# Gated delta rule on one core: inversion blocks on four tiles, recurrence by batch, taps and scaling at other places

## The chip, the core and the metric

One Trainium2 chip, one of its cores. The time is device microseconds (us) of one launch of the kernel. Engines: TensorE (PE; its weight loads are PEld), VectorE (DVE), ScalarE (ACT), GpSimd (POOL) and the queue of SyncE (SP), each with a program of its own, written out by hand, and tied to the others by semaphores.

## The reference

```python
xn = _layernorm(x)                          # x: 4 x 512 x 256
qkv, z, b, a = projections of xn            # 16 key heads, 32 value heads of 128
qkv = silu(causal depthwise conv of 4 taps)
beta = sigmoid(b); g = -exp(A_log) * softplus(a + dt_bias)
# per value head, chunks of 64 positions, g summed within the chunk:
decay = where(tril, exp(g_i - g_j), 0)
M = where(stril, (k_beta @ k.T) * decay, 0)
T = solve_triangular(eye + M, eye)          # inverse of a 64 x 64 matrix
v_c, k_cumdecay = T @ v_beta, T @ (k_beta * exp(g))
# scan over the 8 chunks:
v_new = v_i - kcd_i @ state
out_i = (q_i * exp(g_i)) @ state + attn @ v_new
state = state * exp(g_last) + (k_i * exp(g_last - g_i)).T @ v_new
h = norm_w * rmsnorm(out) * silu(z);  s = h @ W_out.T
y = x + s * silu(ffn of lookup weights)(xn)
```

## The kernel before

The head computes the layer norm, the gates and the first round's inputs; then come 32 rounds, and the feed-forward part as a tail. A round is one key head and two of the four batches (`BB` = 2), so two value heads per batch (`RATIO` = 2), which lie in the two halves of the 128 partitions: a chunk's 64 x 64 matrix of value head 0 in partitions 0 to 63, of value head 1 in 64 to 127. All matmuls are float32; the profile records each as two loads and two matmuls, so 32 matmuls are 64 records. Each engine runs `body(R)`, unrolled six times in a loop of five passes, plus two last rounds; in the last one (`nxt` is False) nothing is prepared for a following round.

The stages of a round on TensorE:

- `invert`: five levels (`LEVELS` - 1). In each, block p1 (`products`: U times W, W is X transposed), then a side matmul, then block p2 (P1 times X), then another (`beside`). The side work of levels 1 to 4 is the projections of the next round, eight in all (`PROJ_AT`: 0 and 1 in level 1, 2 and 3 in level 2, and so on), that of level 5 the gate projections z.
- ScalarE copies p1's result to P1. VectorE copies p2's result into X where a mask says so (`copy_predicated`, in place), and `turn` transposes X into W by 32 x 32 blocks for the next level.
- The projections are raw inputs of the convolution. A kind is two projections, for two batches: kinds 0 to 3 are projections (0, 1), (2, 3), (4, 5), (6, 7). ScalarE's `tap0` writes the first tap to `cacc`, VectorE's `taps` adds three more, reading the projection's bank each time, and then releases both banks; ScalarE's `silu` follows.
- `keys_through`: key products (L475), and the last z.
- `recur`: eight chunks. Kg times state (L510) is added to the old part (L484), VectorE scales it to Vn (L923), Kd times Vn (L537) goes to the state banks, GpSimd's decayed state Sd is added (L931) to give the next St; new part (L490) and qg times state (L518) give the output o. Every two chunks a quarter of the output is ready: ScalarE squares it, GpSimd's `norm` makes its factor, VectorE's `scale_o` multiplies (L943), TensorE's `turn_back` transposes it (L557), VectorE's `gated` multiplies with z (L954).
- `begin` of the following round: kkq products (L422), transposes of k (L430) and v (L435); then `outputs` (L567).

PSUM has eight banks, with a full and a read semaphore each. `bank_uses` lists who uses which bank in a round, in order: a writer waits (`wait_open`) until the use before its own is read. Banks 0, 1, 6, 7 take the projections in turn: projections 0 and 4 share bank 0, 2 and 6 share bank 6. z 0 comes after projection 4 in bank 0. An engine issues in the order of its program, so what stands behind a waiting instruction waits too.

```python
TURN_AT = {3: 0, 5: 1, 7: 2}
PROJ_AT = {lv: (2 * lv - 2, 2 * lv - 1) for lv in range(1, 5)}
```

## Time and profile before

| | |
|---|---|
| median of 3 runs | 3193.22 us |
| lowest, highest | 3192.94, 3195.3 us |
| the profiled execution: its time | 3193.03 us |
| the profiled execution: its span | 3191.2 us |
| TensorE's granted clock, mean over the span | 0.988 |
| one round (first block to first block of the next) | 91.18 us |

Busy times count an engine's own instructions; TensorE's are pipelined and their ends modelled, so starts are what to subtract. In brackets behind a row of a timeline stands how long the engine was idle before it and what released it; DVEq is VectorE's sequencer, which sends a semaphore on. The rounds repeat: the one from 1499.44 to 1590.62 us stands for 31, the last is shown by its own rows.

### The profile page before, as it was taken

The numbers are of one execution on the slowest core, as the hardware profiler recorded it, in microseconds if no ns is written. First come the engines' busy times: TensorE is split into PE (matmuls) and PEld (weight loads), VectorE is DVE, ScalarE is ACT, GpSimd is POOL, SyncE is SP. The second block draws the span as 40 slices with busy tenths as digits, with TensorE's granted clock in tenths as the row PEclk, the third lists the DMA queues.
The fourth block names the chain that finished last, engine by engine and source line by source line (L and its number), as shares of the span: only waits on it lengthen the run. The fifth ranks groups of instructions, "written<-read, shape, count | busy, mean of one in ns | idle before, by whom it ended". The sixth has DMA issues, their size and how long they took to land.

```text
span 3191.2 us, 101541 instructions
## 1 busy us (share of the span) xinstructions
PE 2911.1 (91%) x41680; PEld 2122.0 (66%) x41680; DVE 1643.1 (51%) x2807; ACT 1305.7 (41%) x3046; POOL 1782.0 (56%) x1829
## 2 busy tenths in 40 slices
PE   2899999999999999999999999999999999999889
PEld 1566766766667666667766667677666667766744
DVE  4555555555555555655555555555545655555412
ACT  2443444444444444444444444444444444444311
POOL 1565555656655565665555566655555665555500
PEclk7899999999999999999999999999999999999999
DMA  2111110110111001011110101111011111110020
GB/s 83 27 30 29 30 22 19 27 35 24 30 29 27 20 22 34 24 30 29 30 29 9 35 24 30 30 29 31 13 29 27 29 29 29 30 25 9 3 61 20
DMA packets 71088, 89.52 MB, mean 28 GB/s; under 512 B 16720, under 2 KB 39376, under 8 KB 70608
## 3 DMA queue, kind: packets, MB, share of 16 engines
q1 hardware_dynamic: 70608, 82.74, 10.1%
q8 instruction: 347, 5.69, 0.8%
q14 instruction: 133, 1.09, 0.1%
HBM read 77.64 MB, written 5.08 MB: 26 GB/s over the span
## 4 chain that ended last, share of the span: by engine, by line
issue 35%; POOL 32%; PE 19%; DVE 7%; ACT 2%; POOLq 1%; DVEq 0%; DMA 0%; SPq 0%
POOL hT L1071 10%; POOL hT L1077 5%; PE ps L422 4%; POOL Kd L1094 4%; PE ps_state L537 3%; DVE St L931 3%; PE ps L510 3%; POOL Dm L1012 2%; POOL Sd L1035 2%; POOL Dm L1009 2%; PE ps L557 2%; POOL Kg L1094 2%; PE ps L611 2%; POOL A L1101 1%; PE ps_two L601 1%
## 5 line engine op out<-in xcount | busy, mean ns | idle before, releaser
L1035 POOL TENSOR_TENSOR Sd<-St,el 128x512 f32<-128x512 f32 x192 | 201.3, 1048 | 897.2 <-DVE St L928 843.4
L411 PEld LDWEIGHTS ps<-XW,U 64*64 64x64 f32 x10240 | 317.9, 135 | 125.8 <-issue 123.8
L411 PEld LDWEIGHTS ps<-XW,P 64*64 64x64 f32 x10240 | 311.8, 135 | 119.8 <-issue 119.8
L1071 POOL TENSOR_SCALAR hT<-idx_s,lutb 128x134 f32<-128x134 int32 x480 | 355.4, 744 | 27.5
L411 PE MATMUL ps<-XW,U 64*64 64x64 f32 x10240 | 342.9, 220 | 17.2 <-issue 12.7
L411 PE MATMUL ps<-XW,P 64*64 64x64 f32 x10240 | 333.6, 220 | 0.0
L834 DVE SCALAR_TENSOR_TENSOR cacc<-ps_two,cw,cacc 128x1022 f32<-128x1022 f32 (+2 forms) x192 | 245.7, 1280 | 97.1 <-ACT cacc L638 92.5
L923 DVE TENSOR_TENSOR Vn<-ps,bR 128x256 f32<-128x256 f32 x256 | 108.6, 424 | 350.3 <-PE ps L484 296.7
L834 DVE SCALAR_TENSOR_TENSOR cacc<-ps_state,cw,cacc 128x1022 f32<-128x1022 f32 (+2 forms) x192 | 245.7, 1280 | 78.5 <-ACT cacc L638 73.9
L382 PE MATMUL ps_two<-xnT,w_qkv 128*128 128x512 f32 x512 | 261.8, 636 | 20.4 <-DVEq L838 18.5
L711 ACT ACTIVATE P<-ps 128x512 f32<-128x512 f32 x320 | 184.2, 595 | 229.9 <-PE ps L411 229.3
L382 PE MATMUL ps_state<-xnT,w_qkv 128*128 128x512 f32 x512 | 253.3, 618 | 1.3 <-DVEq L838 1.3
L910 DVE COPY_PREDICATED XW<-cst,ps 128x256 f32<-128x256 int32 x320 | 158.4, 495 | 183.8 <-issue 167.8
L894 DVE STREAM_TRANSPOSE XW<-XW 128x512 f32<-128x512 f32 x320 | 227.7, 711 | 40.5 <-DVE XW L910 9.7
L402 PE MATMUL ps_two<-xnT,w_z 128*128 128x512 f32 x512 | 245.4, 612 | 0.0
L931 DVE TENSOR_TENSOR St<-Sd,ps_state 128x512 f32<-128x512 f32 x192 | 131.9, 687 | 200.1 <-PE ps_state L537 163.9
L567 PE MATMUL ps_two<-w_o,hT 128*128 128x256 f32 x1024 | 226.3, 379 | 0.0
L567 PEld LDWEIGHTS ps_two<-w_o,hT 128*128 128x128 f32 x1024 | 192.1, 190 | 24.8
L510 PE MATMUL ps<-St,Kg 128*64 128x128 f32 x1792 | 146.7, 284 | 58.8 <-DVE St L931 58.6
L537 PE MATMUL ps_state<-Vn,Kd 64*128 64x128 f32 x1792 | 160.3, 295 | 35.4 <-DVE Vn L923 29.9
L422 PE MATMUL ps<-kq 128*128 128x128 f32 x1024 | 132.2, 283 | 62.5 <-DVEq L947 46.6
L738 ACT ACTIVATE P<-ps 128x128 f32<-128x128 f32 x256 | 67.2, 277 | 295.2 <-PE ps L490 295.2
(140 smaller groups left out, 5552.7 us busy)
## 6 DMA issues: line engine op xcount, KB each, us to landing
qg<-g_scratch SPq DMA_DIRECT2D x64, 512.0 KB, 7.4
g_st<-g_scratch SPq DMA_DIRECT2D x64, 256.0 KB, 5.7
w_qkv<-in_wqkvz SPq DMA_DIRECT2D x16, 512.0 KB, 3.8
w_z<-in_wqkvz SPq DMA_DIRECT2D x16, 256.0 KB, 3.1
w_o<-in_wout SPq DMA_DIRECT2D x16, 256.0 KB, 3.3
idx_s<-in_idx SPq DMA_DIRECT2D x32, 67.0 KB, 1.8
fw_scratch<-looked_up SPq DMA_DIRECT2D x32, 67.0 KB, 1.9
Kg<-in_x SPq DMA_DIRECT2D x2, 1024.0 KB, 7.6
```

The costliest lines, as they stand in the source:

```text
L382: m = pe.matmul(bank[:, :], w_qkv[:, k, kind * P:(kind + 1) * P], xnT[:, k, cols(par, b)], start=(k == 0), stop=(k == KD - 1))
L402: m = pe.matmul(bank[:, :], w_z[:, k, a * P:(a + 1) * P], xnT[:, k, cols(R.par, b)], start=(k == 0), stop=(k == KD - 1))
L411: m = pe.matmul(bank[r, c * C:(c + 1) * C], left[r, b, c, :], right[r, b, c, :], start=True, stop=True)
L422: m = pe.matmul(bank[:, u * P:(u + 1) * P], kq[:, i // 2, c, 0:P], kq[:, i // 2, c, C:3 * C], start=True, stop=True)
L510: m = pe.matmul(bank[r, b * P:(b + 1) * P], Kg[:, b, c, r], St[:, cur, b, a, :], start=False, stop=True, skip_group_check=True)
L537: m = pe.matmul(ps[6 + a][:, b * P:(b + 1) * P], Kd[r, b, c, :], Vn[r, cur, b, :], start=True, stop=True)
L567: m = pe.matmul(bank[:, b * D:(b + 1) * D], hT[:, t, b, 1 - a, :], w_o[:, a, :], start=(a == 0), stop=(a == RATIO - 1))
L834: dve.scalar_tensor_tensor(dst, both[n][:, :, 0:S - t], cw[:, kind, 3 - t:4 - t], dst, ALU.mult, ALU.add).then_inc(s["taps"], 1)
L894: dve.transpose(W[:, b].rearrange("p c i -> p (c i)"), X[:, b].rearrange("p c i -> p (c i)")).then_inc(xs, 1)
L931: dve.tensor_tensor(St[:, 1 - cur, :, :, :], Sd[:, :, :, :], part, ALU.add).then_inc(done, 1)
L1035: pool.tensor_tensor(Sd[:, :, :, :], St[:, c % 2, :, :, :], el[:, R.par, :, :, c].unsqueeze(3).broadcast_to([P, BB, RATIO, P]), ALU.mult). ...
L1071: m = pool.tensor_scalar(slots[k], idx_s[:, :], float(k), lutb[:, k:k + 1], ALU.is_equal, ALU.mult)
```

## The change

- `products` issues both batches in one block, on four tiles of 64 x 64. In p1 batch 1 goes to the off-diagonal tiles, so its result lies in swapped halves; p2 takes it from there, and needs X of batch 1 in swapped halves too: the new tile Xs, which ScalarE's `swap` copies (two copies of 64 partitions) after each level's update of X.
- P1's copy, the predicated copy and the transpose cover both batches in one instruction.
- VectorE's `taps` of a kind run one level later (levels 2 to 5, not 1 to 4), ScalarE's `silu` too, the last behind gate 3. The projections stay in their levels and banks.
- In the recurrence each batch has its own bank and its own signals: Vn is two instructions (`tensor_scalar`), the state add two (semaphore `st_c`), and TensorE waits for each batch by itself.
- `scale_o` goes between Vn and the state add of chunks 3, 5, 7, `gated` into the same gap of chunks 4 and 6 and, for the third quarter, into `begin`; `turn_back` stands at the end of chunks 3, 5 and 7. In `begin` scale_o of the last quarter follows all four kkq.
- The mask table `masks` is twice as wide (loaded once, in the head). Banks: kkq in 4 to 7, kt and vt spread over 2 to 7, p1 in 2 and 3, p2 in 4 and 5, outputs o in 2 and 3, their transposes in 1.
- GpSimd: `with_beta` in chunks 1 and 3, `first_level` in 5 and 6, `lengths` (the pow that makes rinv) behind the loop.

VectorE, levels 1 and 2 of a round, before (cacc is written by the taps, with kind 0 in ps_two and kind 1 in ps_state):

```order
L910 COPY_PREDICATED XW<-cst,ps 128x128x2
L911 REGISTER_ALU
L894 STREAM_TRANSPOSE XW<-XW 128x512
L828 ISA
L834 SCALAR_TENSOR_TENSOR cacc<-ps_two,cw,cacc 128x2x511
L832 ISA
L834 SCALAR_TENSOR_TENSOR cacc<-ps_two,cw,cacc 128x2x510
L832 REGISTER_ALU
L834 SCALAR_TENSOR_TENSOR cacc<-ps_two,cw,cacc 128x2x509
L836 REGISTER_ALU
L214 REGISTER_ALU
L909 MEMSET carry 128x1
```

and with the change:

```order
L931 COPY_PREDICATED XW<-cst,ps_p 128x256x2
L933 ISA
L920 STREAM_TRANSPOSE XW<-XW 128x1024
L219 REGISTER_ALU x2
L930 MEMSET carry 128x1
L931 COPY_PREDICATED XW<-cst,ps_p 128x128x4
L933 REGISTER_ALU
L920 STREAM_TRANSPOSE XW<-XW 128x1024
L850 ISA
L856 SCALAR_TENSOR_TENSOR cacc<-ps_two,cw,cacc 128x2x511
```

The taps of kind 0 stood behind level 1's transposes and stand now behind level 2's.

TensorE in chunk 3, before (L557 is turn_back):

```order
L220 REGISTER_ALU
L510 MATMUL ps<-St,Kg 64x128 x4
L518 MATMUL ps<-St,qg 64x128 x4
L557 MATMUL ps<-cst,on 128x2x64 x4
L537 MATMUL ps_state<-Vn,Kd 128x128 x4
L490 MATMUL ps<-Vn,A 64x128
```

and with the change, end of chunk 3 and start of chunk 4 (L501 is the new part, L496 the old, L571 turn_back, L523 Kg times state, L531 qg times state; each L213, L220 or L520 is a wait's number being worked out):

```order
L501 MATMUL ps_p<-Vn,A 64x128
L496 MATMUL ps_p<-V,XW 64x128
L213 REGISTER_ALU
L571 MATMUL ps_two<-cst,on 128x2x64 x4
L520 REGISTER_ALU
L523 MATMUL ps_p<-St,Kg 64x128 x2
L520 REGISTER_ALU
L523 MATMUL ps_p<-St,Kg 64x128 x2
```

The Kg products are two by two, each pair with its wait, and turn_back moved from ahead of the Kd products (L537) to the chunk's end, ahead of the next Kg products.

```diff
-TURN_AT = {3: 0, 5: 1, 7: 2}
+SCALE_AT = {3: 0, 5: 1, 7: 2}
+GATE_AT = {4: 0, 6: 1}
 PROJ_AT = {lv: (2 * lv - 2, 2 * lv - 1) for lv in range(1, 5)}
...
+    begin = (spread([("kkq", i) for i in range(4)], (4, 5, 6, 7)) + spread([("kt", i) for i in range(4)], (2, 4, 5, 6))
+             + spread([("vt", i) for i in range(4)], (3, 7, 2, 4)))
+    levels = []
     for lv in range(1, LEVELS):
-        wide += [("p1", (lv, b)) for b in range(BB)] + [("p2", (lv, b)) for b in range(BB)]
+        levels += spread([("p1", (lv, b)) for b in range(BB)], (2, 3)) + spread([("p2", (lv, b)) for b in range(BB)], (4, 5))
+    small = spread([("z", i) for i in range(4)] + (N2 if nxt else []), (0, 1))
     keys = spread([("kcd", i) for i in range(4)], (4, 5, 6, 7))
-    outs = [("o", 0), ("o", 1), ("ot", 0), ("o", 2), ("ot", 1), ("o", 3), ("ot", 2)]
-    steps = spread([("vn", c) for c in range(NC)] + [("ot3", 0)], (5,)) + spread([("sp", c) for c in range(NC - 1)], (6,))
-    return ahead + spread(small, (0, 1)) + spread(wide, (2, 3, 4)) + keys + spread(outs, (2, 3, 4)) + steps
+    steps = spread([("vn", n) for n in range(NC * BB)], (4, 5)) + spread([("sp", c) for c in range(NC - 1)], (6,))
+    outs = spread([("o", i) for i in range(4)], (2, 3)) + spread([("ot", i) for i in range(4)], (1,))
+    return begin + ahead + levels + small + keys + steps + outs + spread([("out", i) for i in range(4)], (0, 1))
...
-            def products(bank, b, left, right):
...
                 for c in range(NC):
                     for a in range(RATIO):
-                        r = slice(a * C, (a + 1) * C)
-                        m = pe.matmul(bank[r, c * C:(c + 1) * C], left[r, b, c, :], right[r, b, c, :],
-                                      start=True, stop=True)
-                return m
+                        same, other = slice(a * C, (a + 1) * C), slice((1 - a) * C, (2 - a) * C)
+                        cols = slice(c * C, (c + 1) * C)
+                        if first:
+                            left = pe.matmul(banks[0][0][same, cols], U[same, 0, c, :], W[same, 0, c, :], start=True, stop=True)
+                            right = pe.matmul(banks[1][0][other, cols], U[same, 1, c, :], W[same, 1, c, :],
+                                              start=True, stop=True)
+                        else:
+                            left = pe.matmul(banks[0][0][same, cols], P1[same, 0, c, :], X[same, 0, c, :],
+                                             start=True, stop=True)
+                            right = pe.matmul(banks[1][0][same, cols], P1[other, 1, c, :], Xs[other, c, :],
+                                              start=True, stop=True)
+                left.then_inc(banks[0][1], 1)
+                right.then_inc(banks[1][1], 1)
...
-                if last is not None:
-                    turn_back(last, 3)
...
                     m.then_inc(filled, 1)
+                if last is not None:
+                    turn_back(last, 3)
...
                 for lv in range(1, LEVELS):
-                    for b in range(BB):
-                        pe.wait_ge(s["xs"], R.at(3 * (b + 1) if lv == 1 else 6 + (lv - 2) * 4 + 2 * (b + 1), 0, 24))
-                        bank, filled = wait_open(pe, R, "p1", (lv, b))
-                        products(bank, b, U, W).then_inc(filled, 1)
+                    pe.wait_ge(s["xs"], R.at(2 * lv, 0, 11))
+                    products([wait_open(pe, R, "p1", (lv, b)) for b in range(BB)], True)
                     beside(R, lv, 0)
                     for b in range(BB):
                         wait_read(pe, R, "p1", (lv, b))
-                        bank, filled = wait_open(pe, R, "p2", (lv, b))
-                        products(bank, b, P1, X).then_inc(filled, 1)
+                    pe.wait_ge(s["x_c"], R.at(2 * lv, 0, 10))
+                    products([wait_open(pe, R, "p2", (lv, b)) for b in range(BB)], False)
                     beside(R, lv, 1)
...
+                olds = []
                 for b in range(BB):
...
                         m = old_part(R, 0, a, b, bank)
+                    m.then_inc(filled, 1)
+                    olds.append((bank, filled))
                 for c in range(NC):
                     cur = c % 2
-                    if c:
-                        wait_read(pe, R, "sp", c - 1)
                     for b in range(BB if c else 0):
+                        pe.wait_ge(s["st_c"], R.at(2 * (c - 1) + b + 1, 0, 2 * (NC - 1)))
                         for a in range(RATIO):
                             r = slice(a * C, (a + 1) * C)
-                            m = pe.matmul(bank[r, b * P:(b + 1) * P], Kg[:, b, c, r], St[:, cur, b, a, :], start=False,
+                            m = pe.matmul(olds[b][0][r, 0:P], Kg[:, b, c, r], St[:, cur, b, a, :], start=False,
                                           stop=True, skip_group_check=True)
-                    m.then_inc(filled, 1)
+                        m.then_inc(olds[b][1], 1)
...
-                    if c in TURN_AT:
-                        turn_back(R, TURN_AT[c])
...
-                    wait_read(pe, R, "vn", c)
                     if c < NC - 1:
-                        bank, filled = wait_open(pe, R, "vn", c + 1)
                         _, s_filled = wait_open(pe, R, "sp", c)
                         for b in range(BB):
+                            wait_read(pe, R, "vn", c * BB + b)
...
+                                old_part(R, c + 1, a, b, olds[b][0])
...
+                    if c in SCALE_AT:
+                        turn_back(R, SCALE_AT[c])
...
+                swap(R, 0)
...
-                    for b in range(BB):
-                        bank, done = wait_full(act, R, "p1", (lv, b))
-                        src = bank[:, :].rearrange("p (c t) -> p c t", t=C)
-                        act.activation(P1[:, b], src, ACT.Copy).then_inc(done, 1)
-                    if lv < 5:
+                    done = [wait_full(act, R, "p1", (lv, b))[1] for b in range(BB)]
+                    act.activation(P1[:, :, :, :].rearrange("p b c t -> p b (c t)"), ps_p1[:, :, :], ACT.Copy
+                                   ).then_inc(done[0], 1)
+                    wait_read(act, R, "p1", (lv, 0))
+                    act.sem_inc(done[1], 1)
+                    if R.nxt and lv > 2:
+                        silu(R, lv - 3)
+                    if lv < LEVELS - 1:
+                        swap(R, lv)
                         if R.nxt:
-                            if lv > 1:
-                                silu(R, lv - 2)
                             tap0(R, lv - 1)
                     else:
-                        if R.nxt:
-                            silu(R, 3)
                         gate(R, 0)
                         gate(R, 1)
...
+                act.wait_ge(s["xs"], R.at(1 + 2 * lv, 0, 11))
+                for a in range(RATIO):
+                    act.activation(Xs[(1 - a) * C:(2 - a) * C], X[a * C:(a + 1) * C, 1], ACT.Copy).then_inc(s["x_c"], 1)
...
+                    silu(R, 3)
...
                 for i in range(4):
                     if i == 2 and last is not None:
-                        scale_o(last, 3)
+                        gated(last, 2)
...
+                if last is not None:
+                    scale_o(last, 3)
                 for b in range(BB):
-                    if b and last is not None:
-                        gated(last, 3)
                     dve.wait_ge(s["u_c"], R.at(2 * b + 2, 0, 4))
-                    dve.tensor_tensor(X[:, b], X[:, b], over_chunks(eye), ALU.add).then_inc(xs, 2)
-                    dve.wait_ge(xs, R.at(3 * b + 2, 0, 24))
-                    turn(b)
+                over_all = eye.unsqueeze(1).broadcast_to([P, BB * NC, C])
+                x_all = X[:, :].rearrange("p b c i -> p (b c) i")
+                dve.tensor_tensor(x_all, x_all, over_all, ALU.add).then_inc(xs, 1)
+                if last is not None:
+                    gated(last, 3)
+                dve.wait_ge(xs, R.at(1, 0, 11))
+                turn()
...
                 for lv in range(1, LEVELS):
+                    done = [wait_full(dve, R, "p2", (lv, b))[1] for b in range(BB)]
...
+                    dve.memset(carry[:, 1:2], 0.0)
+                    dve.copy_predicated(odd(flat(X)), masks[lv - 1].rearrange("p (q n) -> p q n", n=n).bitcast(I32),
+                                        odd(flat(ps_p2))).then_inc(xs, 1)
+                    dve.wait_ge(xs, R.at(1 + 2 * lv, 0, 11))
                     for b in range(BB):
...
-                        dve.memset(carry[:, 1:2], 0.0)
-                        dve.copy_predicated(dst, mask.bitcast(I32), src).then_inc(xs, 1)
-                        dve.wait_ge(xs, R.at(22 + b + 1 if lv == LEVELS - 1 else 6 + (lv - 1) * 4 + 2 * b + 1, 0, 24))
-                        dve.sem_inc(done, 1)
-                        if lv < LEVELS - 1:
-                            turn(b)
-                    if R.nxt and lv < 5:
-                        taps(R, lv - 1)
+                        dve.sem_inc(done[b], 1)
+                    if lv < LEVELS - 1:
+                        turn()
+                    if R.nxt and lv > 1:
+                        taps(R, lv - 2)
...
-                    bank, done = wait_full(dve, R, "vn", c)
-                    src = bank[:, 0:BB * P].rearrange("p (b e) -> p b e", e=P)
-                    dve.tensor_tensor(Vn[:, cur], src, per_chunk(bR[:, R.par, :, c], P), ALU.mult).then_inc(done, 1)
+                    for b in range(BB):
+                        bank, done = wait_full(dve, R, "vn", c * BB + b)
+                        dve.tensor_scalar(Vn[:, cur, b], bank[:, 0:P], bR[:, R.par, b, c:c + 1], None,
+                                          ALU.mult).then_inc(done, 1)
+                    if c in SCALE_AT:
+                        scale_o(R, SCALE_AT[c])
+                    if c in GATE_AT:
+                        gated(R, GATE_AT[c])
                     if c < NC - 1:
                         _, done = wait_full(dve, R, "sp", c)
-                        part = ps_state[:, :, 0:BB * P].rearrange("p a (b e) -> p b a e", e=P)
-                        if c == 0:
-                            dve.tensor_copy(St[:, 1, :, :, :], part).then_inc(done, 1)
-                        else:
+                        if c:
                             dve.wait_ge(s["sd_c"], R.at(c, 0, NC - 2))
-                            dve.tensor_tensor(St[:, 1 - cur, :, :, :], Sd[:, :, :, :], part, ALU.add).then_inc(done, 1)
+                        for b in range(BB):
+                            part, dst = ps_state[:, :, b * P:(b + 1) * P], St[:, 1 - cur, b, :, :]
+                            if c == 0:
+                                dve.tensor_copy(dst, part).then_inc(s["st_c"], 1)
+                            else:
+                                dve.tensor_tensor(dst, Sd[:, b, :, :], part, ALU.add).then_inc(s["st_c"], 1)
+                        dve.wait_ge(s["st_c"], R.at(2 * c + 2, 0, 2 * (NC - 1)))
+                        dve.sem_inc(done, 1)
                     if c == 0 and R.nxt:
                         lengths(R)
-                    if c in (2, 4, 6):
-                        scale_o(R, c // 2 - 1)
-                    if c in TURN_AT:
-                        gated(R, TURN_AT[c])
...
+                    gated(R, 2)
...
                     decayed_state(R, c)
-                    if c == 1 and R.nxt:
-                        lengths(R)
                     if c % 2 == 0:
                         norm(R, c // 2 - 1)
-                    if R.nxt and c <= BB:
-                        with_beta(R, c - 1)
-                    elif R.nxt and c <= 2 * BB:
-                        first_level(R, c - 1 - BB)
+                    if R.nxt and c in (1, 3):
+                        with_beta(R, c // 2)
+                    elif R.nxt and c > 4:
+                        first_level(R, c - 5)
+                if R.nxt:
+                    lengths(R)
                 norm(R, 3)
```

## Rows read from the trace of the kernel before

**Rows 1.** The page: its first line, and busy time by engine.
```profile
span 3191.2 us, 101541 instructions
...
PE 2911.1 (91%) x41680; PEld 2122.0 (66%) x41680; DVE 1643.1 (51%) x2807; ACT 1305.7 (41%) x3046; POOL 1782.0 (56%) x1829
```

**Rows 2.** Timeline of TensorE, one round: start us, us, engine line op tiles, xcount [idle before].
```profile
1499.44 2.08 PE L411 MATMUL ps<-XW,U 64*64 64x64 f32 x64
1501.45 1.98 PE L382 MATMUL ps_two<-xnT,w_qkv 128*128 128x512 f32 x4
1503.36 2.08 PE L411 MATMUL ps<-XW,P 64*64 64x64 f32 x64
...
1536.99 3.70 PE L402 MATMUL ps_two<-xnT,w_z 128*128 128x512 f32 x8
1540.62 2.00 PE L475 MATMUL ps<-XW,Kg 64*128 64x64 f32 x32
...
1551.95 0.64 PE L510 MATMUL ps<-St,Kg 128*64 128x128 f32 x8
...
1573.28 2.05 PE L422 MATMUL ps<-kq 128*128 128x128 f32 x16 [0.32 <-DVEq L957]
1576.83 2.05 PE L422 MATMUL ps<-kq 128*128 128x128 f32 x16 [1.50 <-DVEq L947]
...
1583.12 0.66 PE L435 MATMUL ps<-cst,vs 128*128 128x128 f32 x4 [0.36 <-ACT V L702]
```

**Rows 3.** Timeline of VectorE, levels 1 and 2 of that round.
```profile
1504.57 0.73 DVE L910 COPY_PREDICATED XW<-cst,ps 128x256 f32<-128x256 int32 x1 [4.34 <-issue]
...
1508.59 3.91 DVE L834 SCALAR_TENSOR_TENSOR cacc<-ps_two,cw,cacc 128x1022 f32<-128x1022 f32 x3 [0.91 <-ACT cacc L638]
1512.85 0.43 DVE L910 COPY_PREDICATED XW<-cst,ps 128x256 f32<-128x256 int32 x1 [0.35 <-DVE cacc L834]
...
1513.43 0.71 DVE L894 STREAM_TRANSPOSE XW<-XW 128x512 f32<-128x512 f32 x1
```

**Rows 4.** Timeline of TensorE, the recurrence: two records on other tiles, and the next group.
```profile
1549.63 0.27 PE L490 MATMUL ps<-Vn,A 64*64 64x128 f32 x1
...
1549.65 0.27 PE L484 MATMUL ps<-V,XW 64*64 64x128 f32 x1
1549.74 0.27 PE L490 MATMUL ps<-Vn,A 64*64 64x128 f32 x1
```

**Rows 5.** Timeline of all engines, levels 1 and 2 of the last round.
```profile
2973.38 0.71 DVE L894 STREAM_TRANSPOSE XW<-XW 128x512 f32<-128x512 f32 x1
...
2974.24 1.15 PE L411 MATMUL ps<-XW,U 64*64 64x64 f32 x32 [0.84 <-DVE XW L894]
...
2975.42 0.60 ACT L711 ACTIVATE P<-ps 128x512 f32<-128x512 f32 x1 [3.32 <-PE ps L411]
```

**Rows 6.** Timeline of TensorE, chunk 4 and the start of chunk 5.
```profile
1561.75 0.66 PE L510 MATMUL ps<-St,Kg 128*64 128x128 f32 x8 [0.27 <-DVE St L931]
...
1563.03 0.71 PE L537 MATMUL ps_state<-Vn,Kd 64*128 64x128 f32 x8 [0.19 <-DVE Vn L923]
...
1564.62 0.66 PE L510 MATMUL ps<-St,Kg 128*64 128x128 f32 x8 [0.27 <-DVE St L931]
```

**Rows 7.** Timeline of VectorE, chunk 4.
```profile
1562.51 0.42 DVE L923 TENSOR_TENSOR Vn<-ps,bR 128x256 f32<-128x256 f32 x1
1563.88 0.69 DVE L931 TENSOR_TENSOR St<-Sd,ps_state 128x512 f32<-128x512 f32 x1 [0.94 <-PE ps_state L537]
```

**Rows 8.** Timeline of GpSimd, the pow that makes rinv.
```profile
1552.43 2.92 POOL L1051 TENSOR_TENSOR rinv<-kn,cst 128x16 f32<-128x16 f32 x1 [1.02 <-DVE kn L852]
```

**Rows 9.** Timeline of TensorE, in the head.
```profile
24.73 1.97 PE L350 MATMUL ps_two<-cst,V 128*128 128x128 f32 x8 [3.41 <-DVE xnT L780]
```

**Rows 10.** Stretches of the head: length, busy time by engine, TensorE's granted clock (PEclk), DMA.
```profile
24.00:28.00 4.00, 3.27 (x15) 2.81 (x16) 2.87 (x6) 0.00 (x0) 0.00 (x0) 1.00 0.00 0
...
40.00:44.00 4.00, 0.00 (x0) 0.00 (x0) 3.82 (x3) 1.40 (x2) 0.00 (x0) 0.50 0.00 0
```

**Rows 11.** The page: the costliest groups, the product blocks on TensorE.
```profile
L411 PE MATMUL ps<-XW,U 64*64 64x64 f32 x10240 | 342.9, 220 | 17.2 <-issue 12.7
L411 PE MATMUL ps<-XW,P 64*64 64x64 f32 x10240 | 333.6, 220 | 0.0
```

46 lines of the change are left out of this document (22 added, 24 removed).

## The prediction

> **What bounds the kernel now.** I read the page first: TensorE is busy for 91% of a span of 3191.2 us, every other engine for 56% or less [rows 1]. In the 40 slices that share never drops between head and tail, so I took one round of 32 from TensorE's timeline and read its idle time. The inversion, from the first product block at 1499.44 to the key products at 1540.62, is 41.18 us without idle time on TensorE: block, projection, block, projection, five times over [rows 2]. A block (both batches, 64 records) starts 2.01 us before the projection behind it, and a projection 1.91 us before the next block [rows 2]. VectorE has slack there: 0.91 us before the taps in level 1, and more before its copies [rows 3]. The recurrence is different: from 1551.95 to 1573.28 (chunks 1 to 7, 21.33 us) TensorE and VectorE hand the work to and fro, 2.87 us from one state product to the next, with two idle gaps on TensorE in each [rows 2, 6, 7]. Behind it the start of the next round stands idle for 1.50 and 0.36 us [rows 2]. So an edit that shortens TensorE's work pays in the inversion only until VectorE's chain binds.
>
> **Blocks on four tiles.** Today two tiles work at a time: 64 records are 32 pairs, 0.06 us apart. In the recurrence four records on four tiles start within 0.02 us, and the next four 0.11 us after the first, with 128 columns each [rows 4]. 64 columns on two tiles take 0.06 us, so the rate per column and tile is the same, and I take 0.06 us for four tiles too: 16 steps fewer, 0.95 us, a block pitch of 1.06 us. The other bound is 0.11 us per group of four, that is, no gain at all. Ten blocks would give 9.5 us per round if TensorE stayed the bound.
>
> The Trainium skill speaks against it: "TensorE: Matmul & The Clock Gate", section "Measured speedup vs the span model", says that a weight load overlaps running matmuls only in another row group, and two of the four tiles share each row group. By that rule a block would keep its 2.0 us; the rows with 128 columns leave room for the tiles to take turns, so this trace does not settle it (a rival below).
>
> **Merged copies.** VectorE's copy and transpose now cover both batches. From 256 to 512 elements an operation grows from 0.42 to 0.69 us [rows 7], 1.05 ns per element. So the predicated copy goes from 0.43 to 0.70 us (0.73 to 1.3 in level 1) and the transpose from 0.71 to 1.25 us; doubled outright they would be 0.86 and 1.42 [rows 3]. 0.15 us lie between them [rows 3] and 0.15 between the transpose's end and TensorE's block [rows 5]. But TensorE can start only when both batches are done. The merged ScalarE copy and the two new Xs copies have a projection to hide behind and a reader one block later; I cost them at nothing, and so the wider mask table, loaded once in the head. Without the projection (last round) they count.
>
> **The taps one level later.** This decides. Projections 4 and 5 of level 3 go into banks 0 and 1, which the taps of kind 0 release. Those taps ran behind level 1's transposes and now run behind level 2's; projection 4 is issued one block after that transpose. The taps take 3.91 us [rows 3], and nothing else on TensorE can pass the waiting projection: block p2 is behind it, and the copy and transpose wait for p2. The same holds in level 4 (banks 6, 7) and level 5 (z into bank 0). With 1.18 us from a one-batch block's start to its reader [rows 5], which a four-tile block matches, the round runs, from its first block:
> level 1: p1 0, projection 1.06, p2 2.97, copy 4.15, transpose 5.60 to 6.85.
> level 2: p1 7.0, projection 8.06, p2 9.97, copy 11.15, transpose 12.0 to 13.25.
> level 3: taps to 17.15, projection 4 at 17.25 (0.1 for the release), p2 19.16, copy 20.34, transpose to 22.45: a period of 9.2 us, where 7.85 is today's (two blocks, two projections).
> level 4: the same, to 31.65.
> level 5: z at 35.65, p2 37.56, the two z behind it 38.6, and 3.63 us later (1536.99 to 1540.62 today) the keys: 42.25.
> That is 1.1 us more than 41.18. The stall of about 2.8 us in three levels eats the whole gain of the blocks.
>
> **Recurrence.** Today's chain in a chunk: Kg product 1561.75, Vn 1562.51, Kd product 1563.03, add 1563.88, next 1564.62 [rows 6, 7]. By batches: Vn of batch 0 can start at 0.48 (half of the eight records fall away) and takes 0.29; batch 1's product starts at 0.35, its Vn ends at 1.13. The qg products stand in between on TensorE and end at 1.10, so the Kd products run from 1.10, the adds start 0.85 later as now, at 1.95, the first (256 elements) takes 0.42, and its batch goes on at 2.42. 0.45 us less. scale_o fits into VectorE's gap before the adds, and gated costs 0.1. But the turn-back transposes of chunks 3 and 5 now stand between the old-part products and the next Kg product: 0.5 us each. I take 2.8 (bR is late in chunk 1), 2.4, 2.9, 2.5, 2.9, 2.5 and 2.4 us: 18.4 against 21.33. 0.1 us goes back in chunk 0, so 2.8 us are gained. The bounds: nothing, if extra waits eat it, and 3.3.
>
> **Start of the next round.** The kkq banks are now 4 to 7, no longer freed by scale_o of the last quarter, and that scale_o stands behind all four. So the idle 1.50 and 0.36 us go [rows 2]: 1.9 us. GpSimd's pow for rinv, 2.92 us [rows 8], now runs before the last norm, which I see ready some 1.5 us ahead of its new reader. If it is late by more than that, the turn-back stalls again; the bound is a gain of 0.
>
> **Sum.** +1.1 - 2.8 - 1.9 = -3.6 us in each of 31 rounds, -112. In the last round nothing fills the levels, and the unsplit chain costs about 1 us more in four levels while the recurrence gives 2.8: +1. The profiled execution took 3193.0 us, 0.2 below the median of the runs, so 3193 - 111 = 3082 us.
>
> **Rivals.**
> 1. Four tiles at 64 columns are no faster than two. Then seven blocks of a round lie on the path (p1 and p2 of levels 1 and 2, p2 of 3 to 5; the other p1 hide under the taps): 7 x 0.95 = 6.6 us on top, +3.0 per round in the sum, +9 in the last: 3295 us, **slower**. It decides from a group pace above about 0.09 us. For it: no row shows four tiles with fewer than 128 columns. Against it: at 128 columns the four start together. Chance 0.10.
> 2. The stalls slow TensorE's clock. After 3.41 us idle it was still granted in full [rows 9, 10]; in another stretch of the head, with no work on TensorE, it was 0.50, the 1.2 GHz level [rows 10]. The new stalls are 2.8 us, with half-filled stretches around. If the projection and block behind each ran at half clock, 3 us x 3 x 31 = 280 us: 3360. Chance 0.05.
> 3. The split by batch gives nothing in the recurrence: 31 x 2.8 = 87 us less gain, 3169. For it: more waits on TensorE in a stretch it already fills, and GpSimd's Sd needs both adds. Chance 0.10.
> 4. The wait for the taps does not bind, as if another bank were free. Then levels 3 to 5 are VectorE's sum, 0.70 + 0.15 + 1.25 + 3.91 + 0.25 = 6.3 us: 3 x 2.9 x 31 = 270 us more gain, 2812. Against it: the bank's counts. Chance 0.04.
>
> **Numbers.** Forecast 3082 us, chance 0.71. Its own bounds: transposes and copies at double length, about 0.2 us in each of nine places on the path, +1.6 per round; half of the recurrence's gain, +1.4; on the other side 1.5 more. That gives 3035 to 3175, which takes in rival 3; left out are rivals 1, 2 and 4, 0.19. A measurement of this kernel can tell 0.2% (6 us) from no change. Faster by more: 0.82. Within: 0.03. Slower: 0.15, rivals 1 and 2.
>
> **What would show it.** TensorE's product groups at half their busy time (342.9 + 333.6 us today [rows 11]), its total near 2570. TensorE idle some 2.8 us before the projection of levels 3 and 4 and before z, released by VectorE's taps. Distance from first block to keys near 42 us, level 3 near 9.2. State products 2.4 us apart, 2.9 where a turn-back stands. No idle 1.5 us between the kkq groups. I am wrong if the blocks still take 2 us, if no wait for taps appears, or if the clock drops behind it.

## The result, and the profile after: slower, though every block is faster

The changed kernel takes 3273.22 us (median of 4 runs, 3264.54 to 3274.49) where the kernel before takes 3194.26 us beside it: ratio 1.0239, 95% interval 1.0219 to 1.0259. The prediction was 3082 us. The profiled execution took 3273.12 us.

The page of the changed kernel, its busy times and two groups of it (line, engine, tiles, count, busy us, mean ns of one, idle us before it and what ended it):

```profile
span 3271.3 us, 103727 instructions
...
PE 2772.6 (85%) x41680; PEld 1898.7 (58%) x41680; DVE 1626.7 (50%) x2775; ACT 1503.5 (46%) x3206; POOL 1803.3 (55%) x1829
...
L387 PE MATMUL ps_two<-xnT,w_qkv 128*128 128x512 f32 x512 | 290.3, 696 | 100.4 <-DVEq L860 98.5
...
L419 PE MATMUL ps_p<-XW,U 64*64 64x64 f32 x5120 | 190.5, 224 | 113.7 <-DVE XW L920 105.1
```

TensorE is busy for 138 us less than before [rows 1], and the span is 80 us longer. So the time is in waits and in slower work, not in more work. The projections show both: 98.5 us of waiting for the taps' release (some 18 us of it are one wait in the head, which the kernel before has too; the rest is 31 waits of 2.6 us), and 290.3 us of busy time for 512 records that took 261.8 before. Their mean went from 636 to 696 ns, though nothing about them was changed.

The start of each round's parts, read from TensorE's timeline over all 32 rounds, says where the 80 us lie. "Inversion" is from the first block p1 to the key products, "rest" from the key products to the next round's first p1.

| us | before | after | difference |
|---|---|---|---|
| start to first p1 | 120.35 | 121.57 | +1.2 |
| inversion, mean of 31 | 41.65 | 48.91 | +7.26 x 31 = +225.1 |
| rest of the round, mean of 31 | 50.25 | 45.26 | -4.99 x 31 = -154.7 |
| inversion of the last round | 29.38 | 39.28 | +9.9 |
| last key products to the end | 192.47 | 191.13 | -1.3 |

The rest of the round gained a little more than the prediction gave it (4.7 us). The inversion lost 7.26 where the prediction had 1.1. Not every round is alike: in the first round of each pass of the loop an inversion takes up to 54.0 us (before, up to 46.6); the others take 47.1 to 49.3 us. VectorE's timeline of one inversion of the changed kernel, whose p1 blocks start at 1536.89, 1544.17, 1550.84, 1561.80 and 1572.75:

```profile
1541.23 1.30 DVE L931 COPY_PREDICATED XW<-cst,ps_p 128x512 f32<-128x512 int32 x1
1542.78 1.25 DVE L920 STREAM_TRANSPOSE XW<-XW 128x1024 f32<-128x1024 f32 x1 [0.24 <-DVE XW L931]
...
1548.51 0.70 DVE L931 COPY_PREDICATED XW<-cst,ps_p 128x512 f32<-128x512 int32 x1
1549.45 1.25 DVE L920 STREAM_TRANSPOSE XW<-XW 128x1024 f32<-128x1024 f32 x1 [0.24 <-DVE XW L931]
1550.62 3.87 DVE L856 SCALAR_TENSOR_TENSOR cacc<-ps_two,cw,cacc 128x1022 f32<-128x1022 f32 x3
...
1559.46 0.70 DVE L931 COPY_PREDICATED XW<-cst,ps_p 128x512 f32<-128x512 int32 x1
...
1570.40 0.71 DVE L931 COPY_PREDICATED XW<-cst,ps_p 128x512 f32<-128x512 int32 x1 [4.96 <-PE ps_p L423]
```

The operations last what was forecast (0.70, 1.30 and 1.25 us). The first period between copies, 7.28 us, is near the forecast 7.0. But the periods behind the taps are 10.95 us and not 9.2, and VectorE itself is idle for 4.96 us in each: it waits for block p2. TensorE's timeline of the same stretch shows the stall and what it does to the projection that follows it:

```profile
1548.27 1.98 PE L387 MATMUL ps_state<-xnT,w_qkv 128*128 128x512 f32 x4
...
1554.60 3.26 PE L387 MATMUL ps_two<-xnT,w_qkv 128*128 128x512 f32 x4 [2.60 <-DVEq L860]
...
1565.56 3.58 PE L387 MATMUL ps_state<-xnT,w_qkv 128*128 128x512 f32 x4 [2.60 <-DVEq L860]
```

The wait itself is the predicted one (2.60 us, forecast 2.8), released by VectorE's taps. The same four records then take 3.26 us instead of 1.98. Stretches of one us through that stall (length, busy time of TensorE, its loads, VectorE, ScalarE and GpSimd, then TensorE's granted clock):

```profile
1552.00:1553.00 1.00, 0.00 (x1) 0.00 (x0) 1.00 (x1) 0.88 (x1) 0.92 (x2) 1.00 0.07 16
1553.00:1554.00 1.00, 0.00 (x0) 0.00 (x0) 0.96 (x2) 0.15 (x1) 0.92 (x2) 1.00 0.00 0
1554.00:1555.00 1.00, 0.40 (x1) 0.30 (x2) 0.49 (x1) 0.41 (x1) 0.92 (x2) 1.00 0.00 0
1555.00:1556.00 1.00, 1.00 (x3) 0.35 (x2) 0.00 (x0) 0.99 (x2) 1.00 (x1) 0.58 0.00 0
1556.00:1557.00 1.00, 1.00 (x3) 0.28 (x1) 0.00 (x0) 0.97 (x2) 0.92 (x2) 0.50 0.00 0
1557.00:1558.00 1.00, 1.00 (x10) 0.22 (x12) 0.00 (x0) 1.00 (x1) 0.92 (x3) 0.50 0.00 0
1558.00:1559.00 1.00, 1.00 (x58) 1.00 (x57) 0.00 (x0) 0.03 (x1) 0.91 (x2) 0.71 0.00 0
1559.00:1560.00 1.00, 1.00 (x22) 0.63 (x15) 0.54 (x2) 0.00 (x0) 0.76 (x2) 1.00 0.08 22
```

The granted clock is still full while TensorE stands idle, and falls to 0.50, the 1.2 GHz level, when the work is just back. At the next stall it falls 0.2 us ahead of the work, at the third (z) 0.9 us ahead. So the price of a stall is paid by the work behind it, the projection and block p2 above all: 1.6, 1.6 and 2.8 us in this round, over the 1.91 and 1.09 us that the two take at full clock. That is what the second rival said; the prediction gave it a chance of 0.05. The Trainium skill describes the pattern ("TensorE: Matmul & The Clock Gate", section "HAM oscillation — how this bites in real kernels"): a kernel that waits once per iteration can start every next piece at half rate. The waits of that section's kernel are longer, some 3 to 5 us, and it has every one of them followed by the low level. Here 2.60 us were enough, but not every time: over the 31 rounds the grant fell at 81 of the 93 stalls and held at 12, all of them in level 3.

These 12 stalls are a comparison inside one kernel, with nothing edited. One of them, and the projection of level 4 behind it:

```profile
328.03 1.98 PE L387 MATMUL ps_two<-xnT,w_qkv 128*128 128x512 f32 x4 [2.60 <-DVEq L860]
...
337.38 3.78 PE L387 MATMUL ps_state<-xnT,w_qkv 128*128 128x512 f32 x4 [2.60 <-DVEq L860]
```

The wait is the same 2.60 us, but the four records take 1.98 us, and level 4's projection follows 9.35 us later, against a forecast period of 9.2. (There the clock falls after all: 3.78 us.) In the 12 rounds where the grant held, this distance is 9.34 to 9.71 us; in the 19 where it fell, 10.68 to 11.98.

### The profile page after: what moved, and what is told of

Its sections match the earlier page's. It is cut to its first block, busy times and chain, and to the rows that moved or that the text cites. A ratio compares the mean times of both kernels' runs of the same rounds, so it can differ in the third digit from the quotient of the medians.

```text
span 3271.3 us, 103727 instructions
## 1 busy us (share of the span) xinstructions
PE 2772.6 (85%) x41680; PEld 1898.7 (58%) x41680; DVE 1626.7 (50%) x2775; ACT 1503.5 (46%) x3206; POOL 1803.3 (55%) x1829
## 4 chain that ended last, share of the span: by engine, by line
PE 64%; DVE 23%; issue 7%; DVEq 1%; ACT 0%; DMA 0%; POOLq 0%; SPq 0%; POOL 0%; ACTq 0%
DVE cacc L856 11%; PE ps_two L407 9%; PE ps_two L581 7%; PE ps_p L423 6%; PE ps_state L387 5%; PE ps_two L387 5%; PE ps_p L523 4%; PE ps_two L399 4%; PE ps_state L547 3%; DVE XW L931 3%; PE ps_p L501 3%; PE ps_two L571 2%; DVE hT L982 2%; PE ps_state L487 2%; PE ps_p L487 2%
## 5 line engine op out<-in xcount | busy, mean ns | idle before, releaser
L387 PE MATMUL ps_two<-xnT,w_qkv 128*128 128x512 f32 x512 | 290.3, 696 | 100.4 <-DVEq L860 98.5
L387 PE MATMUL ps_state<-xnT,w_qkv 128*128 128x512 f32 x512 | 302.7, 722 | 82.1 <-DVEq L860 82.1
L742 ACT ACTIVATE Xs<-XW 64x512 f32<-64x512 f32 x320 | 200.9, 628 | 357.4 <-DVE XW L931 352.5
L423 PEld LDWEIGHTS ps_p<-XW,P 64*64 64x64 f32 x5120 | 201.8, 162 | 182.1 <-issue 182.1
L419 PEld LDWEIGHTS ps_p<-XW,U 64*64 64x64 f32 x5120 | 171.6, 137 | 224.0 <-issue 224.0
L419 PE MATMUL ps_p<-XW,U 64*64 64x64 f32 x5120 | 190.5, 224 | 113.7 <-DVE XW L920 105.1
L946 DVE TENSOR_SCALAR Vn<-ps_p,bR 128x128 f32<-128x128 f32 x512 | 163.9, 348 | 221.7 <-PE ps_p L496 151.1
L724 ACT ACTIVATE P<-ps_p 128x1024 f32<-128x1024 f32 x160 | 163.9, 1024 | 161.9 <-PE ps_p L420 161.9
L423 PE MATMUL ps_p<-XW,P 64*64 64x64 f32 x5120 | 225.1, 250 | 5.8 <-ACTq L727 5.2
L425 PE MATMUL ps_p<-Xs,P 64*64 64x64 f32 x5120 | 225.0, 250 | 0.0
L920 DVE STREAM_TRANSPOSE XW<-XW 128x1024 f32<-128x1024 f32 x160 | 199.3, 1245 | 39.6 <-DVE XW L931 32.6
L425 PEld LDWEIGHTS ps_p<-Xs,P 64*64 64x64 f32 x5120 | 201.5, 162 | 0.0
```

The source lines that it names most:

```text
L387: m = pe.matmul(bank[:, :], w_qkv[:, k, kind * P:(kind + 1) * P], xnT[:, k, cols(par, b)], start=(k == 0), stop=(k == KD - 1))
L419: left = pe.matmul(banks[0][0][same, cols], U[same, 0, c, :], W[same, 0, c, :], start=True, stop=True)
L423: left = pe.matmul(banks[0][0][same, cols], P1[same, 0, c, :], X[same, 0, c, :], start=True, stop=True)
L425: right = pe.matmul(banks[1][0][same, cols], P1[other, 1, c, :], Xs[other, c, :], start=True, stop=True)
L724: act.activation(P1[:, :, :, :].rearrange("p b c t -> p b (c t)"), ps_p1[:, :, :], ACT.Copy).then_inc(done[0], 1)
L742: act.activation(Xs[(1 - a) * C:(2 - a) * C], X[a * C:(a + 1) * C, 1], ACT.Copy).then_inc(s["x_c"], 1)
```

## The experiments

Two theories. **Clock:** the late taps make a stall, the stall lowers TensorE's clock, and the forecast's other terms hold. **Rival:** the levels are long for another reason, such as the order of banks and taps, or four tiles that get in each other's way; the low clock is then only a companion of the waiting.

### Work in the stall: e1_fill and e2_half_fill

Two extra matmuls, or one, keep TensorE at work while it would wait. They write into the bank that block p2 then overwrites, so the result is the same. Below they are called fillers.

```diff
                     products([wait_open(pe, R, "p1", (lv, b)) for b in range(BB)], True)
+                    if R.nxt and lv > 2:
+                        bank, _ = wait_open(pe, R, "p2", (lv, 0))
+                        for k in range(2):
+                            pe.matmul(bank[:, :], ident, xnT[:, k, 0:S], start=True, stop=True)
```

> Theory (the clock): TensorE stands idle some 2.6 us before the projections of levels 3 and 4 and before z, and its clock is then granted at 0.50 for the projection and block behind it, 1.76 + 1.76 + 2.8 us per round in the changed kernel's windows. Two extra matmuls of 512 columns behind block p1 of levels 3 to 5 (1.9 us at full clock, into the bank that p2 overwrites) lie in the wait for the taps, so they are hidden, and leave some 0.9 us idle. The clock should stay at 1.00 there, the periods of levels 3 and 4 fall from 10.96 to about 9.2 us, and the time by 31 x 6.3 = 195 us to some 3080, although TensorE does more work. Rival (the loss has another cause, such as the taps or the banks): the periods stay at 10.96 and the time at 3273, or it grows by up to 31 x 5.7 = 177 us.

> One extra matmul instead of two, 0.95 us, leaves an idle stretch of about 1.9 us. If the clock falls after any stall, the time stays near 3273 + 0; if 1.9 us with the filler before it are short enough, it is as with two, near 3080; in between, only some of the levels fall, and the windows show which.

Measured: 3116.46 us with two (ratio to the kernel before 0.9753, 0.9737 to 0.9769) and 3117.53 us with one (0.9744 to 0.9776). More work made the changed kernel 157 us faster, and faster than the kernel before. Timeline of TensorE with two fillers, a level behind the taps, and stretches of it:

```profile
1563.15 1.98 PE L462 MATMUL ps_p<-xnT,cst 128*128 128x512 f32 x4
1565.82 1.98 PE L387 MATMUL ps_two<-xnT,w_qkv 128*128 128x512 f32 x4 [0.68 <-DVEq L864]
```

```profile
1562.00:1566.00 4.00, 3.26 (x69) 1.92 (x70) 3.63 (x3) 2.11 (x3) 3.61 (x6) 1.00 0.02 4
1566.00:1570.00 4.00, 4.00 (x71) 2.19 (x71) 0.71 (x2) 3.40 (x4) 3.77 (x5) 1.00 0.01 2
```

The projection is back at 1.98 us, at a full grant. VectorE's copies, which show the level's period, lie 9.34 and 9.35 us apart (forecast 9.2):

```profile
1559.72 0.71 DVE L935 COPY_PREDICATED XW<-cst,ps_p 128x512 f32<-128x512 int32 x1
...
1569.06 0.71 DVE L935 COPY_PREDICATED XW<-cst,ps_p 128x512 f32<-128x512 int32 x1 [3.36 <-PE ps_p L423]
...
1578.41 0.71 DVE L935 COPY_PREDICATED XW<-cst,ps_p 128x512 f32<-128x512 int32 x1
```

The mean inversion fell from 48.91 to 43.84 us (31 x 5.07 = 157 us, the whole difference), an ordinary one to 43.0; the rest of the round stayed at 45.28. With one filler the idle piece in front of the projection is 1.54 us, and the grant stays full as well. The price was expected at 195 us from a single round; over all rounds it is 157, or 1.9 us for each of the 81 stalls at which the grant fell. The single round had three such stalls; 12 of the 31 have only two. The rival falls: banks, taps and tiles are as in the changed kernel, and with the grant held the projection is back at its old length.

### Four tiles or two: e3_fill_two_tiles

The blocks are issued as all products of batch 0, then all of batch 1, so that two tiles work at a time, but for the seam between the batches; the fillers stay.

```diff
-                for c in range(NC):
-                    for a in range(RATIO):
...
-                        if first:
...
+                for side in range(2):
+                    for c in range(NC):
+                        for a in range(RATIO):
...
+                            if first and side == 0:
...
+                            elif first:
...
+                            elif side == 0:
```

> The two fillers as before, and each block issued so that only two tiles work at a time (all products of batch 0, then all of batch 1). Four tiles at once were priced at 0.95 us per block. If that is right, the block pitch goes from 1.06 back to 2.0 us, seven blocks of a round lie on the path, and the time is 31 x 6.6 + 9 = 215 us above the kernel with the fillers alone, near 3290. Rival: with p1 longer, the stall before the projection is shorter and TensorE is no bound, so under 4 blocks count, +125 us or less.

Measured: 3262.81 us, 146 above e1_fill. A block's pitch went from 1.09 to 1.84 us (block p1 at 1542.24, filler at 1544.08). So four tiles are worth 0.75 us per block against this kernel, where the block of before, at 2.01 us, is 0.91 above 1.10. The two differ at the seam: here the first records of batch 1 start at 0.77 us, while those of batch 0 go on until 0.93 us, so that four tiles do work there; the 32 pairs of before run one after another throughout. In levels 1 and 2 both blocks count, 1.4 us a level. In levels 3 to 5 the taps cover p1, and 0.6 us a level is left: 31 x 4.42 = 137 us, and 9 in the last round. Both the price of 0.95 and the 125 of the rival were off, one up, one down. The first rival of the prediction (four tiles no faster) is refuted by this pair, as it is by the group pace of 0.06 us in the changed kernel.

### The taps where they were: e4_taps_back

```diff
-                    if R.nxt and lv > 1:
-                        taps(R, lv - 2)
+                    if R.nxt and lv < 5:
+                        taps(R, lv - 1)
```

> VectorE's taps go back to where they were, one level earlier; all else as changed. Theory (the later taps make the stall, the stall lowers the clock): no wait for taps before projections 4, 6 and z, the clock stays at 1.00, first block to keys about 37 us where it is 49.1 now, so 12 x 31 = 372 us less: near 2900. Rival (TensorE is slowed by something else in the changed kernel, or the later stage waits for the taps wherever they are): above 3080.

Measured: 2945.18 us (ratio 0.9217, 0.9202 to 0.9233). One moved line of the change costs 328 us: 157 by the clock (from the changed kernel to e1_fill) and 171 by the wait itself (from e1_fill to here). TensorE's wait for the taps in front of the projections fell from 98.5 to 18.0 us in one group (what is left is the wait in the head) and from 82.1 to 1.4 in the other. An ordinary inversion takes 37.7 us, not the 37 expected, and what bounds it now is VectorE:

```profile
1555.14 0.70 DVE L931 COPY_PREDICATED XW<-cst,ps_p 128x512 f32<-128x512 int32 x1 [0.44 <-DVE cacc L856]
...
1556.08 1.25 DVE L920 STREAM_TRANSPOSE XW<-XW 128x1024 f32<-128x1024 f32 x1 [0.24 <-DVE XW L931]
1558.33 3.91 DVE L856 SCALAR_TENSOR_TENSOR cacc<-ps_state,cw,cacc 128x1022 f32<-128x1022 f32 x3 [1.00 <-ACT cacc L652]
1562.67 0.06 DVE L930 MEMSET carry<- 128x1 f32 x1 [0.44 <-DVE cacc L856]
```

From copy to copy 7.53 us, in which VectorE waits only for its own results and 1.00 us for ScalarE's first tap. The 6.3 us per level that the prediction's fourth rival had for this case leave out that wait and count less for the gaps. On TensorE the idle pieces in front of p1 are 1.45 to 1.51 us, and the grant stays at 1.00 in every us of the round.

### The first tap ahead of the copy to Xs: e5_tap0_first

```diff
-                        swap(R, lv)
                         if R.nxt:
                             tap0(R, lv - 1)
+                        swap(R, lv)
```

> As the kernel with the taps back, and ScalarE writes the first tap before it copies X to Xs. With the taps back a level lasts 7.53 us: copy, 0.24, transpose, 1.00 us of waiting for the first tap, taps 3.91, 0.44, next copy; so VectorE's chain bounds, not TensorE. If so, the first tap can start when the second projection is done, some 3.0 us after block p2, ends 1.1 us later, and a level lasts about 7.2 us: p1 of level 5 comes 1.85 us earlier, 57 us in all, near 2890. Rival: the later Xs copy makes block p2 wait, and nothing or a loss is left, 2945 or more.

Measured: 2896.13 us (ratio 0.9065, 0.905 to 0.908), 6 us above what was expected. The wait for the first tap shrinks in the later levels, to 0.46 us here, and a level to 7.0:

```profile
1535.24 0.72 DVE L931 COPY_PREDICATED XW<-cst,ps_p 128x512 f32<-128x512 int32 x1 [0.43 <-DVE cacc L856]
...
1537.90 3.91 DVE L856 SCALAR_TENSOR_TENSOR cacc<-ps_two,cw,cacc 128x1022 f32<-128x1022 f32 x3 [0.46 <-ACT cacc L652]
1542.25 0.75 DVE L931 COPY_PREDICATED XW<-cst,ps_p 128x512 f32<-128x512 int32 x1 [0.43 <-DVE cacc L856]
```

### The recurrence without the split: e6_no_split

```diff
-                        pe.wait_ge(s["st_c"], R.at(2 * (c - 1) + b + 1, 0, 2 * (NC - 1)))
+                        pe.wait_ge(s["st_c"], R.at(2 * c, 0, 2 * (NC - 1)))
...
                         for b in range(BB):
                             wait_read(pe, R, "vn", c * BB + b)
+                        for b in range(BB):
...
+                    vn = [wait_full(dve, R, "vn", c * BB + b) for b in range(BB)]
                     for b in range(BB):
-                        bank, done = wait_full(dve, R, "vn", c * BB + b)
+                        bank, done = vn[b]
```

> As the kernel with the taps back (2945 us), but the recurrence's signals are joined again: TensorE waits for both batches' states before the first Kg product and for both Vn before the first Kd product, VectorE for both Kg products before the first Vn. The moved scaling and turn-back stay. The prediction's working gave the split by batch 0.45 us per chunk: 7 x 0.45 x 31 = 98 us more, near 3043. Rival: the recurrence's gain (18.6 us where it was 21.3) comes from the moved scaling, and the split gives nothing: 2945.

Measured: 3041.43 us, 96 us above e4_taps_back where 98 were expected. VectorE's chunk now shows a wait for the Kg products ahead of Vn:

```profile
1564.52 0.61 DVE L948 TENSOR_SCALAR Vn<-ps_p,bR 128x128 f32<-128x128 f32 x2 [0.93 <-PE ps_p L523]
```

With the split the same row reads:

```profile
1597.46 0.67 DVE L946 TENSOR_SCALAR Vn<-ps_p,bR 128x128 f32<-128x128 f32 x2 [0.22 <-PE ps_p L523]
```

The rest of the round takes 48.11 us instead of 45.20 (31 x 2.91 = 90), and the last recurrence and what follows 6 us more. So the split by batch carries the recurrence's gain (2.91 us a round, where the whole gain was forecast at 2.8), and the third rival falls.

### The turn-back ahead again: e7_turn_early

```diff
+                if last is not None:
+                    turn_back(last, 3)
                 for i in range(4):
                     bank, filled = wait_open(pe, R, "kt", i)
...
-                if last is not None:
-                    turn_back(last, 3)
                 for i in range(4):
                     bank, filled = wait_open(pe, R, "vt", i)
```

> As the kernel with the taps back, but the turn-back of the last quarter stands ahead of the transposes of k again. There it waits for its scaling: the transposes would be done by then, 2.2 us of TensorE, and stand behind it now, so about 1.9 us per round, 60 us, near 3005. Rival: the transposes' place doesn't matter, since something later (VectorE's X) ends last before the next round's first block: 2945.

Measured: 3026.57 us, 81 us above e4_taps_back where 60 were expected. The stall cost the rest of the round 1.8 us in some rounds (46.8 us) and 3.4 in others (48.4). In one of the latter:

```profile
1573.28 1.11 PE L571 MATMUL ps_two<-cst,on 128*128 128x128 f32 x4 [2.05 <-DVE on L971]
1574.18 2.72 PE L445 MATMUL ps_p<-cst,kq 128*128 128x128 f32 x12
```

```profile
1572.00:1573.00 1.00, 0.00 (x0) 0.00 (x0) 1.00 (x3) 0.69 (x2) 1.00 (x2) 1.00 0.67 166
1573.00:1574.00 1.00, 0.72 (x4) 0.72 (x5) 0.68 (x2) 0.00 (x0) 1.00 (x2) 0.66 0.79 180
1574.00:1575.00 1.00, 1.00 (x6) 1.00 (x5) 1.00 (x2) 0.00 (x0) 1.00 (x1) 0.50 0.84 162
```

The wait is about the expected one (2.05 us; its cost was put at 1.9), and the rounds at 46.8 us show that cost alone. The same twelve transposes take 2.72 us here where they take 1.47 at full clock. A stall of the same length in the same place lowered the clock in 17 of 31 rounds; at 1.6 us each that is some 27 us, enough for the 21 beyond what was expected.

### Block p2 ahead of the waiting projection: e8_p2_first

The changed kernel's late taps, with the order on TensorE changed in levels 3 to 5.

```diff
-                    beside(R, lv, 0)
+                    if lv < 3:
+                        beside(R, lv, 0)
...
                     products([wait_open(pe, R, "p2", (lv, b)) for b in range(BB)], False)
+                    if lv > 2:
+                        beside(R, lv, 0)
                     beside(R, lv, 1)
```

> The changed kernel with its late taps, but in levels 3 to 5 block p2 is issued before the projection that waits for them, and both projections follow it. If the loss is that p2 stands behind the waiting projection in TensorE's order, the wait is gone: TensorE has p1 1.09, some 1.5 idle for P1's copy, p2 1.09, two projections 3.82, 7.5 us per level where the fillers gave 9.35, and in level 5 9.4 where they gave 10.4: 4.7 us per round under the kernel with fillers (3116), near 2970, at a clock of 1.00. Rival: the taps bind wherever the projection stands, and the idle stretches bring the clock down: 3116 or more.

Measured: 3021.63 us. The wait for the taps is gone, as expected, but 50 us of the expected gain are missing. An inversion takes mostly 40.6 us where 38.3 were expected. TensorE in level 4, and two stretches of it:

```profile
1520.68 0.24 PE L423 MATMUL ps_p<-XW,P 64*64 64x64 f32 x1 [2.36 <-ACTq L730]
1522.42 4.64 PE L387 MATMUL ps_state<-xnT,w_qkv 128*128 128x512 f32 x8
```

```profile
1520.00:1521.00 1.00, 0.32 (x19) 0.35 (x22) 0.00 (x0) 0.82 (x2) 1.00 (x2) 0.97 0.27 67
1521.00:1522.00 1.00, 1.00 (x52) 1.00 (x47) 0.00 (x0) 1.00 (x1) 0.92 (x2) 0.50 0.07 19
```

ScalarE's copy of P1 is late there, because it stands behind the silu operations, the copy to Xs and the first tap on its engine. That makes an idle piece of 2.36 us instead of 1.5, and the clock falls again: eight records of projections in 4.64 us, 3.8 at full clock. It happens in level 4 alone, where 21 of 25 such pieces (2.19 to 2.45 us) brought the clock down; in levels 3 and 5 the piece is 1.66 us, and the grant mostly held. So the queue position was the cause of the wait, and the same effect came back by another engine.

### The last round: e9_fill_last

On top of e5_tap0_first, one filler behind each block p1 and p2 of the last round alone.

```diff
                     beside(R, lv, 0)
+                    if not R.nxt and lv < 5:
+                        filler(wait_open(pe, R, "p2", (lv, 0))[0])
...
                     beside(R, lv, 1)
+                    if not R.nxt and lv < 5:
+                        filler(wait_open(pe, R, "p1", (lv + 1, 0))[0])
```

> The fastest kernel so far (2896 us), with one extra matmul of 512 columns behind each block p1 and each block p2 of the last round alone, where there are no projections: it has idle stretches of 1.3 and 2.5 us in every level, a clock of 0.50, and 7.8 us from one level to the next, where the chain at full clock is 2.45 us from p1 to p2 and 3.7 us from there to the next p1. If the clock is the cause here too, a level comes down to about 6.2 us, the last inversion from 40.7 to some 33.5 us, and the time to 2889. Rival: these levels wait for VectorE and ScalarE at any clock, and the extra matmuls bring nothing, 2896, or stand in the way, up to 2903.

Measured: 2889.15 us (ratio 0.9034, 0.9022 to 0.9046), the fastest of all. The last inversion fell from 40.74 to 32.99 us, although it does more work. A stretch of it without the fillers and then with them:

```profile
2676.00:2684.00 8.00, 3.97 (x128) 3.65 (x128) 2.15 (x4) 2.45 (x4) 7.37 (x10) 0.50 0.01 2
```

```profile
2676.00:2684.00 8.00, 6.26 (x194) 3.73 (x185) 1.96 (x3) 3.09 (x4) 7.37 (x10) 1.00 0.02 4
```

## Why the prediction was wrong

- **The four tiles**: right. Block to projection 1.10 us (forecast 1.06), at the changed kernel's own rows. The Trainium skill's rule that the prediction weighed against it ("TensorE: Matmul & The Clock Gate"; it stands in the section "The mechanism", not in the one that the prediction names) would, as read there, have kept 2.0 us. The trace does not agree with it for this block.
- **The merged operations**: sizes right (0.70, 1.30, 1.25 us). The gaps were small by a little: 0.24 us between copy and transpose, not 0.15, and 1.34 us from p2's start to its copy, not 1.18. Level by level they add up to 0.75 us a round: with the clock held an ordinary inversion takes 43.0 us, and 42.25 was forecast. That is 23 us. The mean over all rounds is 43.84, 2.19 above before, where 1.1 was forecast: 34 us in all, which is the distance from 3082 to e1_fill. The other 11 us lie mostly in the first rounds of the loop's passes (48.0 to 48.4 us with the fillers, 43.2 to 46.6 before), which the prediction, worked out from one ordinary round, did not treat apart.
- **The late taps**: the place (projections 4 and 6, and z 0), the releaser and the length of the wait (2.60 us, forecast 2.8) were right.
- **The recurrence and the start of the round**: -4.99 us a round, forecast -4.7. In the round read it was 18.61 us from chunk 1 to the next kkq products (forecast 18.4), and e6 and e7 show that the split by batch carries the one and the moved turn-back the other.
- **The last round**: forecast +1 in all, from +4 in the inversion and -2.8 behind it; measured +9.9 and -1.3. Behind an idle piece of 3.11 us the grant falls to 0.50 there, and with pieces of 2.52 and 1.31 us in every level it stays down, which the term left out; e9 shows that work in these pieces brings the full clock back.
- **The step that failed** is the sum's unstated one, that TensorE works at full clock behind a stall of 2.8 us, and with it the chance of 0.05 for the second rival. The prediction's own last sign of being wrong, that the clock drops behind the wait, is the one that came. The rival's price was 280 us, from three waits with projection and block at half clock for their whole length. Measured are 157 (e1_fill), 5.1 us a round: the projection loses 1.3 to 1.8 us and not 1.9, and the block 0 to 0.8 and not 1.1, since the grant is at 0.50 for a part of them only, and at 12 of the 93 stalls it does not fall at all. The forecast of 3082, plus 34 for the gaps and the first rounds of the passes, plus 157 for the clock, makes 3273, as measured. The smaller terms beside them, -9 for the rest of the rounds, +8 for the last round and +1 ahead of the first block, cancel.

The reason for the low chance was one row: 3.41 us idle in the head with a full grant behind it [rows 9, 10]. The stretches beside it are 4 us wide, and the one in which the grant fell, from 36 to 40 us, is not among those shown. In steps of 1 us the trace of before also shows the opposite. The eight transposes that start at 35.72 end at 36.8, and the grant falls within the second us after them:

```profile
37.00:38.00 1.00, 0.00 (x0) 0.00 (x0) 0.51 (x1) 0.45 (x1) 0.00 (x0) 1.00 0.00 0
38.00:39.00 1.00, 0.00 (x0) 0.00 (x0) 0.76 (x2) 0.98 (x2) 0.00 (x0) 0.61 0.00 0
39.00:40.00 1.00, 0.00 (x0) 0.00 (x0) 0.10 (x1) 0.99 (x2) 0.00 (x0) 0.50 0.00 0
```

One row where it held and one where it fell are no ground for 0.05.

## What to carry to other kernels

When a change puts a wait of a few us on TensorE, price what stands behind it at half clock as a case of its own weight; look in the trace for every place where the grant fell, in stretches of 1 us, before arguing from one where it held. A wait that recurs in every iteration can be filled with matmuls whose result is thrown away, or the work behind it can be taken in another order: against the changed kernel fillers gave 157 us here, block p2 ahead of the waiting projection 252, and taking the wait away 328. And after a merge, read the whole queue of the helping engine: the order of two operations on ScalarE was worth 49 us.

## What the runs showed of the hardware

- The grant does not follow the length of the idle piece alone. It fell at 81 of 93 pieces of about 2.6 us (the changed kernel), 21 of 25 of 2.19 to 2.45 us and 4 of 61 of 1.65 to 1.70 us (both e8_p2_first), and 17 of 31 of about 2.05 us (e7_turn_early). It held at all 93 of about 1.54 us (e2_half_fill), and in the head behind 3.41 us. No run here isolates what decides.
- It can fall late: at the 81 stalls between 1.4 us ahead of the returning work and 1.3 us behind its start, and behind it in 32 of them. So an idle stretch read by itself can show a full grant. The busy times of unchanged work are where the loss shows (projections 696 and 722 ns in the mean, 636 and 618 before).
- Four 64 x 64 tiles started within 0.02 us of each other and took a new group every 0.06 us, with the weights of the next group loaded meanwhile.
- Merging two operations on VectorE saved little: a transpose of 1024 elements takes 1.25 us where two of 512 took 1.42.
